# One stage for a whole gated recurrent mixer: norms, five projections, scan and output projection, batch by batch

## The chip, the core and the metric

The kernel runs on one core of a Trainium2 chip. TensorE (PE, with its weight loads PEld) multiplies matrices, VectorE (DVE), ScalarE (ACT) and GpSimd (POOL) work element by element, SyncE (SP) issues the transfers. Each engine runs its own instructions in order and waits on semaphores. The metric is the time of one execution on the device in microseconds.

## What is computed

The model has two layers of two mixers and a feed-forward part each, on x of 4 batches x 512 positions x 256 features. Every part is added to x after a layer norm. The change touches the second mixer of layer 2 alone:

```
xn = layernorm(x)                                   # the mixer's input, also its residual
y  = xn * rsqrt(mean(xn*xn) + 1e-5) * rms_w
f  = sigmoid(y @ Wf.T + bf)
z  = (y @ Wz.T) * sigmoid(y @ Wzg.T)
h_t = f_t * h_(t-1) + z_t                           # along the 512 positions, in bfloat16
gated = bfloat16(silu(y @ Wga.T) * (y @ Wgb.T)) * h
x  = x + gated @ Wout.T + bout + xn
```

## The kernel before

All activations stay in SBUF: X (rows: 128 positions x 16 tiles x 256 features, float32), XN (its norm) and XT (features on the partitions: 2 tiles x 2048 positions). A batch is 4 tiles of rows (TB), or 512 columns of XT. The kernel is a row of stages. Each `Stage` has its own buffers, semaphores and one block with a program for each engine; at its end the semaphores are cleared and all engines meet at a barrier, so nothing of a stage overlaps the next. Within an engine the order is the one written out by hand.

The mixer takes five stages (from the end of `hybrid_kernel`):

- `layer_norm` "ln7": VectorE takes statistics of a batch (L90, L93, L96), GpSimd the power -0.5 (L113), VectorE scales X into XN (L103), TensorE transposes it (L121) and ScalarE copies it into XT (L130). The mixer does not use this XT.
- `rms_scale`: VectorE squares XN (L1082), reduces all 16 tiles (L1084), GpSimd takes the power (L1077), VectorE scales XN into XR (L1089).
- `turn`: TensorE transposes XR (L397), ScalarE and VectorE copy the banks in turn (L406, L413).
- `recurrence`: SP loads the five weights, rms_w and the bias of f (L1117 to L1119). VectorE multiplies the transposed rows by rms_w (L1164). For each of eight units n (batch n // 2, half n % 2 of the 256 hidden features) TensorE makes five banks (f, z, z's gate, ga, gb), each of two float32 matmuls of 512 columns, which the trace shows as four records (L1138). ScalarE makes f and the two sigmoids (L1148, L1153); VectorE makes z (L1169), gg = ga * sigmoid(ga) (L1173) and gate (L1176). When all eight are done VectorE runs the eight scans (L1180) and products go (L1184), each copied to XT by ScalarE (L1156).
- `project_add` "r_out": SP loads the weight and the bias row (L428, L430). VectorE adds XN and then the bias to X (L448, L454), TensorE multiplies each tile of rows (L439), VectorE adds it (L459).

The helper class `Norm` is there already and used by another stage. Of it the change uses `statistics` and `scale`, which issue for one batch what L90 to L103 issue in `layer_norm`, with semaphores vare, rst and xn.

The experts' stage that follows (`moe2`) begins with a layer norm of X (lines L90 to L130 again).

Other lines named in the rows: L1734, L1782 are elementwise work of layer 2's first mixer, L2227 and L2263 too (L2227 a GpSimd product of two SBUF tiles, L2263 a VectorE product of two SBUF tiles), L814 the down projection of the shared expert.

Of the kernel before, what the change touches and what calls it, by code (L numbers as in the profile page):

```python
# [12 lines left out]
P = 128  # L13
# [1047 lines left out]

def rms_scale(nc, name, XN, XR, eps):

    with Stage(nc, name) as s:
        ms = s.sb("meansq", [P, NT])
        r = s.sb("r", [P, NT])
        mhalf = s.sb("mhalf", [P, NT])
        sq = s.sb("sq", [P, NT, DM])
        squared, msd, rd, out, half = (s.sem(n) for n in ("squared", "meansq", "r", "out", "half"))
        blk = s.block()  # L1070

        @blk.gpsimd
        def _(pool):
            nc.gpsimd.memset(mhalf[:, :], -0.5).then_inc(half, 1)
            pool.wait_ge(half, 1)
            pool.wait_ge(msd, 2)
            nc.gpsimd.tensor_tensor(r[:, :], ms[:, :], mhalf[:, :], ALU.pow).then_inc(rd, 1)  # L1077

        @blk.vector
        def _(dve):  # L1080
            for t in range(NT):
                nc.vector.tensor_tensor(sq[:, t, :], XN[:, t, :], XN[:, t, :], ALU.mult).then_inc(squared, 1)  # L1082
            dve.wait_ge(squared, NT)
            nc.vector.tensor_reduce(ms[:, :], sq[:, :, :], AX, ALU.add).then_inc(msd, 1)  # L1084
            dve.wait_ge(msd, 1)
            nc.vector.tensor_scalar(ms[:, :], ms[:, :], 1.0 / DM, eps, ALU.mult, ALU.add).then_inc(msd, 1)
            dve.wait_ge(rd, 1)
            for t in range(NT):
                nc.vector.tensor_scalar(XR[:, t, :], XN[:, t, :], r[:, t:t + 1], None, ALU.mult).then_inc(out, 1)  # L1089


def recurrence(nc, name, XRT, rms_w, w5, bf, GT):

# [4 lines left out]
    with Stage(nc, name) as s:  # L1098
        w = s.sb("w", [P, KT, 5 * DM])
        rw = s.sb("rms_w", [P, KT])  # L1100
        b_f = s.sb("bf", [P, 2])
        f = s.sb("f", [P, R, SEQ], BF16)
        z = s.sb("z", [P, R, SEQ], BF16)
        gate = s.sb("gate", [P, R, SEQ], BF16)
        h = s.sb("h", [P, R, SEQ], BF16)
        sig = s.sb("sig", [P, 2, 2, SEQ])
        gg = s.sb("gg", [P, 2, SEQ])
        go = s.sb("go", [P, R, SEQ], BF16)
        bank = [s.ps(f"bank{i}") for i in range(5)]
        ld, scaled, made, f_s, sig_s = (s.sem(n) for n in ("loaded", "scaled", "made", "f", "sig"))  # L1110
        zs, ggs, gs, steps, gos, outs = (s.sem(n) for n in ("z", "gg", "gate", "step", "go", "out"))
        blk = s.block()
        F_, Z, ZG, GA_, GB = range(5)

        @blk.sync
        def _(sp):
            sp.dma_start(w[:, :, :], tiles(w5)).then_inc(ld, 16)  # L1117
            sp.dma_start(rw[:, :], rms_w).then_inc(ld, 16)
            sp.dma_start(b_f[:, :], bf).then_inc(ld, 16)  # L1119
# [21 lines left out]

        @blk.scalar
        def _(act):
            act.wait_ge(ld, 48)
            for n in range(R):
# [8 lines left out]
            for n in range(R):  # L1154
                act.wait_ge(gos, n + 1)
                nc.scalar.copy(GT[:, n % 2, (n // 2) * SEQ:(n // 2 + 1) * SEQ], go[:, n, :]).then_inc(outs, 1)  # L1156

        @blk.vector
        def _(dve):
            dve.wait_ge(ld, 48)  # L1160
            for b in range(BATCH):
                for k in range(KT):
                    x = XRT[:, k, b * SEQ:(b + 1) * SEQ]
                    nc.vector.tensor_scalar(x, x, rw[:, k:k + 1], None, ALU.mult).then_inc(scaled, 1)  # L1164
            for n in range(R):
# [3 lines left out]
                nc.vector.tensor_tensor(z[:, n, :], bank[Z][:, :], sig[:, j, 0, :], ALU.mult).then_inc(zs, 1)  # L1169
                dve.wait_ge(sig_s, 2 * n + 2)  # L1170
                if n >= 2:
                    dve.wait_ge(gs, n - 1)
                nc.vector.tensor_tensor(gg[:, j, :], bank[GA_][:, :], sig[:, j, 1, :], ALU.mult).then_inc(ggs, 1)  # L1173
                dve.wait_ge(made, 5 * n + GB + 1)
                dve.wait_ge(ggs, n + 1)
                nc.vector.tensor_tensor(gate[:, n, :], gg[:, j, :], bank[GB][:, :], ALU.mult).then_inc(gs, 1)  # L1176
            for n in range(R):
                dve.wait_ge(f_s, n + 1)
                dve.wait_ge(zs, n + 1)
                nc.vector.tensor_tensor_scan(h[:, n, :], f[:, n, :], z[:, n, :], 0.0, ALU.mult, ALU.add  # L1180
                                             ).then_inc(steps, 1)
# [1323 lines left out]
```

## Time and profile before

| | |
|---|---|
| median of 3 runs | 4703.91 us (4699.47 to 4708.26) |
| the profiled execution | 4706.56 us, its span 4704.8 us |
| TensorE busy, share of the span | 4118.0 us, 88% |
| VectorE | 2696.7 us, 57% |
| ScalarE | 2268.6 us, 48% |
| GpSimd | 630.6 us, 13% |
| mean granted clock of TensorE | 0.919 of full speed |

Times in the trace are microseconds from the start of the span. A float32 matmul shows as two records, each with a weight load. "x20" behind a row means that 20 instructions in a row are merged, and what stands in square brackets is the idle time before it and what ended it. A record's length includes its way through the engine, so that the next of the same kind can start earlier: what a row of them costs is the distance of their starts.

### The profile page before, as it was taken

The numbers are of one execution on the slowest core, as the hardware profiler recorded it, in microseconds if no ns is written. First come the engines' busy times: TensorE is split into PE (matmuls) and PEld (weight loads), VectorE is DVE, ScalarE is ACT, GpSimd is POOL, SyncE is SP. The second block draws the span as 40 slices with busy tenths as digits, with TensorE's granted clock in tenths as the row PEclk, the third lists the DMA queues.
The fourth block names the chain that finished last, engine by engine and source line by source line (L and its number), as shares of the span: only waits on it lengthen the run. The fifth ranks groups of instructions, "written<-read, shape, count | busy, mean of one in ns | idle before, by whom it ended". The sixth has DMA issues, their size and how long they took to land. (4 is left out here: it accounts for less than half of the span.)

```text
span 4704.8 us, 79644 instructions
## 1 busy us (share of the span) xinstructions
PE 4118.0 (88%) x27938; PEld 2752.2 (58%) x27938; DVE 2696.7 (57%) x7063; ACT 2268.6 (48%) x6183; POOL 630.6 (13%) x557
## 2 busy tenths in 40 slices
PE   5988988888797799959999999999999999977667
PEld 3555545555555566646666666666766666644344
DVE  3663357777623788856666665566556666423342
ACT  1551146666411566635556555656565565522111
POOL 0000010000000344421111111111111111111011
PEclk8788989889897899979999999999999999979879
DMA  2000100000000655553222332333233232121012
GB/s 70 1 1 24 51 1 2 2 2 2 4 27 5 206 200 205 213 134 84 79 70 74 84 84 71 81 84 83 70 84 84 66 80 79 37 92 57 11 34 76
DMA packets 402161, 318.92 MB, mean 68 GB/s; under 512 B 289200, under 2 KB 339056, under 8 KB 399728
## 3 DMA queue, kind: packets, MB, share of 16 engines
q1 hardware_dynamic: 398704, 305.53, 22.6%
q0 software_dynamic: 3072, 8.39, 0.6%
q8 instruction: 225, 3.69, 0.3%
q14 instruction: 160, 1.31, 0.1%
HBM read 195.94 MB, written 117.88 MB: 67 GB/s over the span
## 5 line engine op out<-in xcount | busy, mean ns | idle before, releaser
L2153 ACT ACTIVATE d_heads_VP<-d_heads_chain,d_GALL 128x128 f32<-128x128 f32 x512 | 187.9, 367 | 665.1 <-PE d_heads_chain L2055 663.5
L2299 DVE SCALAR_TENSOR_TENSOR d_heads_S<-d_heads_S,d_GALL,d_heads_chain 128x128 f32<-128x128 f32 x768 | 232.4, 344 | 436.0 <-PE d_heads_chain L2060 435.9
L599 ACT ACTIVATE b_heads_PR<-b_heads_sc,b_heads_NM 128x384 f32<-128x384 f32 (+3 forms) x512 | 273.0, 535 | 203.4 <-DVE b_heads_NM L667 203.4
L1763 DVE SCALAR_TENSOR_TENSOR d_front_CY<-d_front_proj,d_CW,d_front_CY 128x511 f32<-128x511 f32 (+2 forms) x384 | 274.1, 745 | 72.6 <-ACT d_front_CY L1681 68.0
L1969 PE MATMUL d_heads_value<-all_XT,d_heads_WVZ 128*128 128x512 f32 x512 | 271.1, 612 | 27.9 <-DMA d_heads_WVZ<-w_d_qkvz 27.9
L2232 POOL TENSOR_TENSOR d_heads_RM<-d_heads_MS,d_heads_mhalf 128x4 f32<-128x4 f32 x128 | 130.4, 1019 | 1199.9 <-DVE d_heads_MS L2312 1199.9
L2277 DVE SCALAR_TENSOR_TENSOR d_heads_CY<-d_heads_value,d_CW,d_heads_CY 128x511 f32<-128x511 f32 (+2 forms) x384 | 284.6, 741 | 1.8
L1990 PE MATMUL d_heads_value<-d_heads_WVZ,all_XT 128*128 128x256 f32 x1024 | 273.6, 390 | 12.0 <-DVE d_heads_CY L2277 12.0
L2087 PE MATMUL d_heads_projected<-d_heads_WO,d_heads_OT 128*128 128x256 f32 x1024 | 277.0, 394 | 0.7 <-ACT d_heads_OT L2172 0.7
L2060 PE MATMUL d_heads_chain<-d_heads_VP,d_heads_KD 64*128 64x128 f32 x1792 | 220.4, 322 | 54.2 <-ACT d_heads_VP L2153 54.1
L2291 DVE SCALAR_TENSOR_TENSOR d_heads_UU<-d_heads_chain,d_GALL,d_heads_VB 128x128 f32<-128x128 f32 x448 | 156.5, 349 | 192.9 <-PE d_heads_chain L2042 192.9
L547 PEld LDWEIGHTS b_heads_tp<-all_ident,b_heads_PR 128*128 128x128 f32 x1280 | 158.0, 156 | 170.7 <-ACT b_heads_PR L599 129.1
L2042 PE MATMUL d_heads_chain<-d_heads_S,d_heads_KQ 128*64 128x128 f32 x1792 | 249.3, 302 | 8.5 <-DVE d_heads_S L2299 2.4
L547 PE MATMUL b_heads_tp<-all_ident,b_heads_PR 128*128 128x128 f32 x1280 | 223.6, 311 | 37.2 <-DVE b_heads_PT L679 24.3
L1639 PE MATMUL d_front_proj<-all_XT,d_front_WKQ 128*128 128x512 f32 x512 | 242.4, 618 | 15.3 <-DMA d_front_WKQ<-w_d_qkvz 15.3
L2065 PE MATMUL d_heads_output<-d_heads_VP,d_heads_ITB 128*128 128x128 f32 x1024 | 244.4, 321 | 0.0
L538 PE MATMUL b_heads_sc<-b_QKT,b_heads_QM 32*128 32x128 f32 (+3 forms) x1024 | 229.3, 527 | 17.0 <-DVE b_heads_QM L635 8.9
L2060 PEld LDWEIGHTS d_heads_chain<-d_heads_VP,d_heads_KD 64*128 64x128 f32 x1792 | 134.8, 184 | 176.9 <-ACT d_heads_VP L2153 163.7
L2227 POOL TENSOR_TENSOR d_heads_QS<-d_heads_KQ,d_heads_GE 128x512 f32<-128x512 f32 x128 | 162.9, 1274 | 517.2 <-PE d_heads_output L2065 510.8
L2045 PE MATMUL d_heads_output<-d_heads_S,d_heads_QS 128*64 128x128 f32 x1792 | 226.8, 282 | 0.0
L2263 DVE TENSOR_TENSOR d_heads_TMP<-d_heads_INV 128x30 f32<-128x30 f32 (+14 forms) x480 | 209.5, 437 | 28.5 <-DMA d_heads_INV<-d_l 25.1
L2042 PEld LDWEIGHTS d_heads_chain<-d_heads_S,d_heads_KQ 128*64 128x64 f32 x1792 | 126.7, 136 | 158.5 <-DVE d_heads_S L2299 56.2
(323 smaller groups left out, 8932.3 us busy)
## 6 DMA issues: line engine op xcount, KB each, us to landing
d_kq<-d_front_KQ SPq DMA_DIRECT2D x64, 768.0 KB, 4.3
d_heads_KQ<-d_kq SPq DMA_DIRECT2D x64, 768.0 KB, 4.9
d_heads_GE<-d_gerows SPq DMA_DIRECT2D x128, 256.0 KB, 5.3
d_front_GR<-d_grows SPq DMA_DIRECT2D x32, 512.0 KB, 6.4
d_it<-d_front_LI SPq DMA_DIRECT2D x64, 256.0 KB, 2.1
d_l<-d_front_LI SPq DMA_DIRECT2D x64, 256.0 KB, 4.0
d_heads_ITB<-d_it SPq DMA_DIRECT2D x128, 128.0 KB, 2.8
d_heads_INV<-d_l SPq DMA_DIRECT2D x256, 32.0 KB
```

The source lines that it names most:

```text
L547: mm = nc.tensor.transpose(TP[j][:, k * P:(k + 1) * P], PR[p % 3][j][:, k * P:(k + 1) * P], C.ident[:, :])
L599: nc.scalar.activation(PR[p % 3][j][:, 0:width(p)], SC[p % 2][j][:, 0:width(p)], ACT.Exp, bias=NM[:, u % 2, t, slot:slot + 1], scale=-1.0 ...
L1639: mm = nc.tensor.matmul(FB[2 * (i % 2) + c][:, :], WKQ[:, k, g, col:col + HD], XT[:, k, b * SEQ:(b + 1) * SEQ], start=(k == 0), stop=(k == ...
L1763: stt(y, FB[2 * (i % 2) + c][:, 0:SEQ - j], CW[:, n, 3 - j:4 - j], y, ALU.mult, ALU.add).then_inc(convstep if j < 3 else convs, 1)
L1969: mm = nc.tensor.matmul(BV[h][:, :], w[:, k, h * HD:(h + 1) * HD], XT[:, k, b * SEQ:(b + 1) * SEQ], start=(k == 0), stop=(k == KT - 1))
L1990: mm = nc.tensor.matmul(BV[t // 2][:, (t % 2) * DM:(t % 2 + 1) * DM], XT[:, k, b * SEQ + t * P:b * SEQ + (t + 1) * P], w[:, k, 2 * HD:4 * HD],
L2042: mm = nc.tensor.matmul(R[0][hrows(h), 0:HD], kq[:, c, 0, :], S[:, h, :], start=True, stop=True)
L2060: mm = nc.tensor.matmul(R[h][:, HD:2 * HD], KD[i % 2][hrows(h), c, :], VP[c % 2][hrows(h), :], start=True, stop=True)
L2065: mm = nc.tensor.matmul(inter, ITB[i % 2][:, c, :], VP[c % 2][:, :], start=(c == 0), stop=True, skip_group_check=True)
L2087: mm = nc.tensor.matmul(BO[:, t * DM:(t + 1) * DM], OT[:, h, t * P:(t + 1) * P], WO[g % 2][:, h, :], start=(h == 0), stop=(h == 1))
L2277: stt(y, BV[h][:, 0:SEQ - j], CW[:, 2 * HK + 2 * g + h, 3 - j:4 - j], y, ALU.mult, ALU.add).then_inc(convstep if j < 3 else convs, 1)
L2299: stt(S[:, h, :], S[:, h, :], gate(i, GEL0 + h, c), R[h][:, HD:2 * HD], ALU.mult, ALU.add).then_inc(su, 1)
```

## The change

`gated_scan` replaces the five stages. All of it is one stage with one block, and its order goes by batches. Both norms are made of the statistics of X: with variance v and r = 1/sqrt(v + 1e-5) the mean square of the normed row is v * r * r, so the second factor is (v r r + 1e-5)^-0.5, and XR = (X - mean) * (r * factor) comes straight from X. XN is still made, for the residual. rms_w is ScalarE's scale in the copy of the transposed rows. The two adds of the residual and the bias go to GpSimd, one batch behind the norms. The scan of a unit stands in VectorE's order between its gg and its gate; the output projection of a batch stands behind the projections of the next one, two tiles of rows in a bank of PSUM, added with one instruction. TensorE has one bank for each of the five projections as before, two for the transposes and one for the output.

Lines that are only "..." stand for what is left out, the bodies of the two removed functions above all (they are in the kernel before).

```diff
     return M
-def rms_scale(nc, name, XN, XR, eps):
...
+def gated_scan(nc, name, X, XN, GT, W, C):
+    R = 2 * BATCH
     with Stage(nc, name) as s:
...
+        w, wo = s.sb("w", [P, KT, 5 * DM]), s.sb("w_out", [P, KT, DM])
+        rw, b_f, b_o = s.sb("rms_w", [P, KT]), s.sb("bf", [P, 2]), s.sb("bias", [P, DM])
+        XR, XRT = s.sb("rows", [P, NT, DM]), s.sb("rows_turned", [P, KT, NT * P])
+        SQ, RR, RS = (s.sb(n, [P, NT]) for n in ("meansq", "root", "factor"))
+        f, z, gate, h, go = (s.sb(n, [P, R, SEQ], BF16) for n in ("f", "z", "gate", "h", "go"))
+        sig, gg = s.sb("sig", [P, 2, 2, SEQ]), s.sb("gg", [P, 2, SEQ])
+        xp = [s.ps(f"xp{i}") for i in range(2)]
+        bank = [s.ps(f"bank{i}") for i in range(5)]
+        ob = s.ps("out_bank")
+        N = Norm(nc, s, X, XN, None, C, xp)
+        (wl, bl, ol, tiny, sqd, rrd, rsd, xr, turned, copied, made, f_s, sig_s, zs, ggs, gs, steps, gos, outs, op, added, biased,
+         res) = (s.sem(n) for n in (
+             "weights_loaded", "bias_loaded", "out_loaded", "tiny", "meansq", "root", "factor", "rows", "turned", "copied", "made",
+             "f", "sig", "z", "gg", "gate", "scanned", "gated", "go_copied", "out_made", "added", "biased", "residual"))
         blk = s.block()
+        F_, Z, ZG, GA_, GB = range(5)
+        out_bank = lambda u: xp[0] if u == 2 * BATCH - 1 else ob
+        @blk.sync
+        def _(sp):
+            sp.dma_start(w[:, :, :], tiles(W["r_w5"])).then_inc(wl, 16)
+            sp.dma_start(rw[:, :], W["rms_w"]).then_inc(bl, 16)
+            sp.dma_start(b_f[:, :], W["Wf_b"]).then_inc(bl, 16)
+            sp.dma_start(b_o[:, :], W["r_out_bias"].broadcast_to([P, DM])).then_inc(ol, 16)
+            sp.dma_start(wo[:, :, :], tiles(W["r_out"])).then_inc(ol, 16)
         @blk.gpsimd
         def _(pool):
...
-def recurrence(nc, name, XRT, rms_w, w5, bf, GT):
...
+            nc.gpsimd.memset(N.mhalf[:, :], -0.5).then_inc(N.half, 1)
+            pool.wait_ge(N.half, 1)
+            def residual(b):
+                own = slice(b * TB, (b + 1) * TB)
+                pool.wait_ge(N.xn, TB * (b + 1))
+                pool.wait_ge(xr, TB * (b + 1))
+                pool.wait_ge(ol, 32)
+                nc.gpsimd.tensor_tensor(XN[:, own, :], XN[:, own, :], b_o[:, :].unsqueeze(1).broadcast_to([P, TB, DM]), ALU.add
+                                        ).then_inc(biased, 1)
+                pool.wait_ge(biased, b + 1)
+                nc.gpsimd.tensor_tensor(X[:, own, :], X[:, own, :], XN[:, own, :], ALU.add).then_inc(res, 1)
+            for b in range(BATCH):
+                own = slice(b * TB, (b + 1) * TB)
+                pool.wait_ge(N.vare, b + 1)
+                nc.gpsimd.tensor_tensor(N.rstd[:, own], N.var[:, own], N.mhalf[:, own], ALU.pow).then_inc(N.rst, 1)
+                pool.wait_ge(sqd, b + 1)
+                nc.gpsimd.tensor_tensor(RR[:, own], SQ[:, own], N.mhalf[:, own], ALU.pow).then_inc(rrd, 1)
+                if b >= 1:
+                    residual(b - 1)
+            residual(BATCH - 1)
         @blk.tensor
         def _(pe):
...
-            for n in range(R):
...
+            def turn_rows(b):
+                pe.wait_ge(xr, TB * (b + 1))
+                for k in range(KT):
+                    if b > 0:
+                        pe.wait_ge(copied, 2 * (b - 1) + k + 1)
+                    for t in range(TB):
+                        mm = nc.tensor.transpose(xp[k][:, t * P:(t + 1) * P], XR[:, TB * b + t, k * P:(k + 1) * P],
+                                                 C.ident[:, :])
+                    mm.then_inc(turned, 1)
+            def project_five(n):
+                b, j = divmod(n, 2)
+                pe.wait_ge(copied, 2 * (b + 1))
                 for q in range(5):
                     if n > 0:
                         if q == F_:
                             pe.wait_ge(f_s, n)
-                        elif q in (Z, ZG):
+                        elif q == Z:
                             pe.wait_ge(zs, n)
+                        elif q == ZG:
+                            pe.wait_ge(sig_s, 2 * n - 1)
                         elif q == GA_:
                             pe.wait_ge(ggs, n)
                         else:
@@ -1139,10 +1147,42 @@
                                               XRT[:, k, b * SEQ:(b + 1) * SEQ], start=(k == 0), stop=(k == KT - 1))
                     mm.then_inc(made, 1)
+            def project_out(u):
+                pe.wait_ge(outs, 2 * (u // 2 + 1))
+                pe.wait_ge(ol, 32)
+                if u == 2 * BATCH - 1:
+                    pe.wait_ge(copied, 2 * BATCH)
+                else:
+                    pe.wait_ge(added, u)
+                for i in range(2):
+                    t = 2 * u + i
+                    for k in range(KT):
+                        mm = nc.tensor.matmul(out_bank(u)[:, i * DM:(i + 1) * DM], GT[:, k, t * P:(t + 1) * P], wo[:, k, :],
+                                              start=(k == 0), stop=(k == KT - 1))
+                mm.then_inc(op, 1)
+            turn_rows(0)
+            pe.wait_ge(wl, 16)
+            for b in range(BATCH):
+                project_five(2 * b)
+                if b + 1 < BATCH:
+                    turn_rows(b + 1)
+                if b >= 1:
+                    project_out(2 * b - 2)
+                project_five(2 * b + 1)
+                if b >= 1:
+                    project_out(2 * b - 1)
+            project_out(2 * BATCH - 2)
+            project_out(2 * BATCH - 1)
         @blk.scalar
         def _(act):
...
-            for n in range(R):
+            def copy_rows(b):
+                for k in range(KT):
+                    act.wait_ge(turned, 2 * b + k + 1)
+                    nc.scalar.activation(XRT[:, k, b * SEQ:(b + 1) * SEQ], xp[k][:, :], ACT.Copy, scale=rw[:, k:k + 1]
+                                         ).then_inc(copied, 1)
+            def gates(n):
                 j = n % 2
                 act.wait_ge(made, 5 * n + F_ + 1)
                 nc.scalar.activation(f[:, n, :], bank[F_][:, :], ACT.Sigmoid, bias=b_f[:, j:j + 1]).then_inc(f_s, 1)
@@ -1151,37 +1191,78 @@
                     if n >= 2:
                         act.wait_ge(zs if i == 0 else ggs, n - 1)
                     nc.scalar.activation(sig[:, j, i, :], bank[q][:, :], ACT.Sigmoid).then_inc(sig_s, 1)
-            for n in range(R):
+            def copy_gated(n):
                 act.wait_ge(gos, n + 1)
                 nc.scalar.copy(GT[:, n % 2, (n // 2) * SEQ:(n // 2 + 1) * SEQ], go[:, n, :]).then_inc(outs, 1)
+            act.wait_ge(bl, 32)
+            copy_rows(0)
+            for b in range(BATCH):
+                gates(2 * b)
+                if b + 1 < BATCH:
+                    copy_rows(b + 1)
+                if b >= 1:
+                    copy_gated(2 * b - 1)
+                gates(2 * b + 1)
+                copy_gated(2 * b)
+            copy_gated(R - 1)
         @blk.vector
         def _(dve):
...
-            for n in range(R):
+            def norm(b):
+                own = slice(b * TB, (b + 1) * TB)
+                N.statistics(dve, b)
+                dve.wait_ge(N.rst, b + 1)
+                nc.vector.tensor_tensor(SQ[:, own], N.rstd[:, own], N.rstd[:, own], ALU.mult).then_inc(tiny, 1)
+                dve.wait_ge(tiny, 2 * b + 1)
+                nc.vector.tensor_tensor(SQ[:, own], SQ[:, own], N.mv[:, own, 1], ALU.mult).then_inc(tiny, 1)
+                dve.wait_ge(tiny, 2 * b + 2)
+                nc.vector.tensor_scalar_add(SQ[:, own], SQ[:, own], 1e-5).then_inc(sqd, 1)
+                N.scale(dve, b)
+                dve.wait_ge(rrd, b + 1)
+                nc.vector.tensor_tensor(RS[:, own], RR[:, own], N.rstd[:, own], ALU.mult).then_inc(rsd, 1)
+                dve.wait_ge(rsd, b + 1)
+                for t in range(b * TB, (b + 1) * TB):
+                    nc.vector.tensor_scalar(XR[:, t, :], X[:, t, :], N.mv[:, t, 0:1], RS[:, t:t + 1], ALU.subtract, ALU.mult
+                                            ).then_inc(xr, 1)
+            def gates(n):
                 j = n % 2
                 dve.wait_ge(made, 5 * n + Z + 1)
                 dve.wait_ge(sig_s, 2 * n + 1)
                 nc.vector.tensor_tensor(z[:, n, :], bank[Z][:, :], sig[:, j, 0, :], ALU.mult).then_inc(zs, 1)
+                dve.wait_ge(made, 5 * n + GA_ + 1)
                 dve.wait_ge(sig_s, 2 * n + 2)
                 if n >= 2:
                     dve.wait_ge(gs, n - 1)
                 nc.vector.tensor_tensor(gg[:, j, :], bank[GA_][:, :], sig[:, j, 1, :], ALU.mult).then_inc(ggs, 1)
+                dve.wait_ge(f_s, n + 1)
+                dve.wait_ge(zs, n + 1)
+                nc.vector.tensor_tensor_scan(h[:, n, :], f[:, n, :], z[:, n, :], 0.0, ALU.mult, ALU.add).then_inc(steps, 1)
                 dve.wait_ge(made, 5 * n + GB + 1)
                 dve.wait_ge(ggs, n + 1)
                 nc.vector.tensor_tensor(gate[:, n, :], gg[:, j, :], bank[GB][:, :], ALU.mult).then_inc(gs, 1)
-            for n in range(R):
...
                 dve.wait_ge(gs, n + 1)
                 dve.wait_ge(steps, n + 1)
                 nc.vector.tensor_tensor(go[:, n, :], gate[:, n, :], h[:, n, :], ALU.mult).then_inc(gos, 1)
+            def add(u):
+                dve.wait_ge(res, u // 2 + 1)
+                dve.wait_ge(op, u + 1)
+                x = X[:, 2 * u:2 * u + 2, :].rearrange("p t n -> p (t n)")
+                nc.vector.tensor_tensor(x, x, out_bank(u)[:, :], ALU.add).then_inc(added, 1)
+            norm(0)
+            for b in range(BATCH):
+                if b + 1 < BATCH:
+                    norm(b + 1)
+                gates(2 * b)
+                if b >= 1:
+                    add(2 * b - 2)
+                gates(2 * b + 1)
+                if b >= 1:
+                    add(2 * b - 1)
+            add(2 * BATCH - 2)
+            add(2 * BATCH - 1)
@@ -2417,14 +2498,7 @@
             M.load = None
-            layer_norm(nc, "ln7", X, XN, XT, C)
-            with Stage(nc, "r") as a:
-                XR = a.sb("XR", [P, NT, DM])
-                rms_scale(nc, "r_rms", XN, XR, 1e-5)
-                XRT = a.sb("XRT", [P, KT, NT * P])
-                turn(nc, "r_turn", XR, XRT, C)
-                recurrence(nc, "r_scan", XRT, W["rms_w"], W["r_w5"], W["Wf_b"], XT)
-            project_add(nc, "r_out", X, XT, W["r_out"], bias_row=W["r_out_bias"], residual=XN)
+            gated_scan(nc, "r", X, XN, XT, W, C)
             experts(nc, "moe2", X, XN, XT, W, M, C)
         store_x(nc, X, out)
```

## Rows read from the trace of the kernel before

**Rows 1.** the page's head

```profile
span 4704.8 us, 79644 instructions
```

**Rows 2.** the table by stretches (us, busy time (x instructions) of each engine, clock, DMA)

```profile
4337.50:4389.10 51.60, 13.86 (x65) 12.49 (x65) 32.74 (x98) 7.04 (x12) 7.89 (x7) 0.53 0.07 26
4389.10:4460.60 71.50, 71.46 (x160) 31.19 (x160) 15.87 (x24) 16.33 (x25) 0.00 (x0) 0.96 0.00 0
4460.60:4496.10 35.50, 15.50 (x64) 13.11 (x64) 28.75 (x41) 4.94 (x8) 0.00 (x0) 0.76 0.05 12
```

**Rows 3.** timeline from 4337 us (start, length, engine, line, operation)

```profile
4337.52 1.41 DVE L90 BATCH_NORM_STATS2 ln_stats<-all_X 128x6 f32<-128x256 f32 x4 [0.95 <-PEq L40]
...
4339.57 1.05 POOL L113 TENSOR_TENSOR ln_rstd<-ln_var,ln_mhalf 128x4 f32<-128x4 f32 x1 [1.97 <-DVE ln_var L96]
...
4341.11 1.38 DVE L103 TENSOR_SCALAR all_XN<-all_X,ln_meanvar,ln_rstd 128x256 f32<-128x256 f32 x4
...
4344.54 0.59 ACT L130 COPY all_XT<-ln_xp 128x512 f32<-128x512 f32 x1 [0.27 <-PE ln_xp L121]
```

**Rows 4.** DMA issues from 4337 to 4497 us (KB, us to landing)

```profile
r_scan_w<-w_r_w SPq DMA_DIRECT2D x1, 1280.0 KB, 5.5
```

**Rows 5.** groups of instructions from 4337 to 4497 us (busy us, mean ns)

```profile
L1138 PE MATMUL r_scan_bank<-r_XRT,r_scan_w 128*128 128x512 f32 x160 | 71.5, 610 | 10.8 <-DVE r_XRT L1164 10.8
...
L439 PE MATMUL r_out_bank<-r_out_w,all_XT 128*128 128x256 f32 x64 | 15.5, 407 | 19.6 <-DMA r_out_bias<-w_r_out_bias 19.6
...
L1156 ACT CAST all_XT<-r_scan_go 128x512 f32<-128x512 bf16 x8 | 4.9, 618 | 10.8 <-DVE r_scan_go L1184 10.8
```

**Rows 6.** timeline of TensorE's weight loads from 4389 us

```profile
4392.61 0.34 PEld L1138 LDWEIGHTS r_scan_bank<-r_XRT,r_scan_w 128*128 128x128 f32 x1 [0.52 <-issue]
4393.47 0.34 PEld L1138 LDWEIGHTS r_scan_bank<-r_XRT,r_scan_w 128*128 128x128 f32 x1 [0.52 <-issue]
4394.31 0.19 PEld L1138 LDWEIGHTS r_scan_bank<-r_XRT,r_scan_w 128*128 128x128 f32 x1 [0.50 <-issue]
```

**Rows 7.** timeline of the old turn's bank copies from 4374.5 us

```profile
4376.54 0.59 ACT L406 COPY r_XRT<-r_turn_bank 128x512 f32<-128x512 f32 x1 [1.12 <-PE r_turn_bank L397]
4377.39 0.69 DVE L413 COPY r_XRT<-r_turn_bank 128x512 f32<-128x512 f32 x1 [1.01 <-PE r_turn_bank L397]
4377.82 0.59 ACT L406 COPY r_XRT<-r_turn_bank 128x512 f32<-128x512 f32 x1 [0.70 <-PE r_turn_bank L397]
```

**Rows 8.** timeline of VectorE from 4459 us

```profile
4459.51 0.69 DVE L1173 TENSOR_TENSOR r_scan_gg<-r_scan_bank,r_scan_sig 128x512 f32<-128x512 f32 x1 [0.95 <-ACT r_scan_sig L1153]
4460.60 0.69 DVE L1176 TENSOR_TENSOR r_scan_gate<-r_scan_gg,r_scan_bank 128x512 bf16<-128x512 f32 x1 [0.40 <-PE r_scan_bank L1138]
4461.20 1.22 DVE L1180 TENSOR_TENSOR_SCAN r_scan_h<-r_scan_f,r_scan_z 128x512 bf16<-128x512 bf16 x1
4462.53 0.43 DVE L1184 TENSOR_TENSOR r_scan_go<-r_scan_gate,r_scan_h 128x512 bf16<-128x512 bf16 x1
```

**Rows 9.** timeline of GpSimd and VectorE from 3005 us

```profile
3005.74 1.27 POOL L2227 TENSOR_TENSOR d_heads_QS<-d_heads_KQ,d_heads_GE 128x512 f32<-128x512 f32 x1
3006.04 1.01 DVE L2263 TENSOR_TENSOR d_heads_TMP<-d_heads_INV 128x30 f32<-128x30 f32 x1
...
3009.25 0.21 DVE L2263 TENSOR_TENSOR d_heads_TMP<-d_heads_INV 128x58 f32<-128x58 f32 x1
```

**Rows 10.** timeline from 1752 us, and line L113 by min/median/max ns

```profile
1752.10 4.05 POOL L1734 TENSOR_TENSOR d_front_LI<-d_front_LI,d_front_NB 128x512 f32<-128x512 f32 x4
...
1753.66 1.28 DVE L1782 TENSOR_TENSOR d_front_LI<-d_front_kk,d_front_D 128x512 f32<-128x512 f32 x2
...
L113 POOL TENSOR_TENSOR ln_rstd<-ln_var,ln_mhalf x4: 1047/1244/1247, 4339.6 to 4347.4; 128x4 f32<-128x4 f32 x4
```

**Rows 11.** timeline of TensorE from 4325 us

```profile
4325.27 1.13 PE L814 MATMUL moe_bank<-moe_shared_down,moe_hid 128*128 128x256 f32 x4 [0.54 <-DVE all_X L999]
4329.50 2.07 PE L814 MATMUL moe_bank<-moe_shared_down,moe_hid 128*128 128x256 f32 x4 [3.10 <-issue]
```

More of the change, by code:

```diff
@@ L1059, in expert_weights @@
     return M
-def rms_scale(nc, name, XN, XR, eps):
+def gated_scan(nc, name, X, XN, GT, W, C):
+    R = 2 * BATCH
     with Stage(nc, name) as s:
[L1065 to L1069, printed above, removed]
-        blk = s.block()
+        w, wo = s.sb("w", [P, KT, 5 * DM]), s.sb("w_out", [P, KT, DM])
[12 more added lines that the diff above has]
+             "f", "sig", "z", "gg", "gate", "scanned", "gated", "go_copied", "out_made", "added", "biased", "residual"))
+        blk = s.block()
+        F_, Z, ZG, GA_, GB = range(5)
[7 more added lines that the diff above has]
+            sp.dma_start(wo[:, :, :], tiles(W["r_out"])).then_inc(ol, 16)
@@ L1072, in _ @@
         @blk.gpsimd
         def _(pool):
[L1074 to L1089, printed above, removed]
@@ L1092, in recurrence @@
-def recurrence(nc, name, XRT, rms_w, w5, bf, GT):
-    R = 2 * BATCH
[L1098 to L1119, printed above, removed]
+            nc.gpsimd.memset(N.mhalf[:, :], -0.5).then_inc(N.half, 1)
@@ L1122, in _ @@
         def _(pe):
-            pe.wait_ge(ld, 48)
-            pe.wait_ge(scaled, R)
-            for n in range(R):
-                b, j = n // 2, n % 2
+            def turn_rows(b):
[7 more added lines that the diff above has]
+                    mm.then_inc(turned, 1)
@@ L1140, in _ @@
                     mm.then_inc(made, 1)
+            def project_out(u):
[24 more added lines that the diff above has]
+            project_out(2 * BATCH - 1)
         @blk.scalar
         def _(act):
-            act.wait_ge(ld, 48)
-            for n in range(R):
+            def copy_rows(b):
[4 more added lines that the diff above has]
+            def gates(n):
                 j = n % 2
@@ L1153, in _ @@
                     nc.scalar.activation(sig[:, j, i, :], bank[q][:, :], ACT.Sigmoid).then_inc(sig_s, 1)
-            for n in range(R):
+            def copy_gated(n):
                 act.wait_ge(gos, n + 1)
                 nc.scalar.copy(GT[:, n % 2, (n // 2) * SEQ:(n // 2 + 1) * SEQ], go[:, n, :]).then_inc(outs, 1)
+            act.wait_ge(bl, 32)
[9 more added lines that the diff above has]
+            copy_gated(R - 1)
         @blk.vector
         def _(dve):
[L1160 to L1164, printed above, removed]
-            for n in range(R):
+            def norm(b):
[15 more added lines that the diff above has]
+            def gates(n):
                 j = n % 2
@@ L1176, in _ @@
                 nc.vector.tensor_tensor(gate[:, n, :], gg[:, j, :], bank[GB][:, :], ALU.mult).then_inc(gs, 1)
-            for n in range(R):
[L1178 to L1181, printed above, removed]
                 dve.wait_ge(gs, n + 1)
```

## The prediction

> **What bounds the kernel now.** I read the page's head first: the profiled execution spans 4704.8 us [rows 1]. Then the table by stretches. The changed mixer is three stretches of 158.6 us in all [rows 2]: 51.6 us from the first statistics of its layer norm to the first projection matmul, 71.5 us of projections, 35.5 us from the last projection to the last add. In the first TensorE is busy 13.9 us and VectorE 32.7, in the third TensorE is busy 15.5 and VectorE 28.7: no engine is full there, the stages stand one behind the other. In the middle TensorE is busy 71.46 of 71.50 us: that is a floor. The other 4546 us of the kernel aren't touched. So the question is how much of 51.6 + 35.5 = 87.1 us goes beside the 71.5 us, and what TensorE work comes into its path in return.
>
> **The front.** I take the timeline of the old norm as the pattern [rows 3]. Statistics of a batch and their pow on GpSimd: 4337.52 to 4340.62, so 3.1 us. New behind it: three chained tiny VectorE instructions; the small ones in this trace cost 0.17 to 0.21 us, I take 0.2 each, 0.6. Then the second pow, 1.24 us, beside which the four XN scalings run (1.38 us for four [rows 3]); RS, another 0.2; the four scalings into XR, 1.4, as they have the form of the XN ones; all with hops 3.6. That puts XR of batch 0 at 6.7 us. From the last XN to the second ScalarE copy the old timeline takes 4342.49 to 4345.13, 2.65 us [rows 3], eight transposes among it; the copy now carries rms_w as its scale, which takes the eight multiplies (L1164) away. First projection matmul at 9.4 us instead of 51.55: 42.1 us saved. The four stage boundaries that go are within these stretches. Cover: the weights (1280 KB, 5.5 us to landing [rows 4]) are issued at the stage's start and needed at 9.4; if they came after that, every us would show. SP issues the same five transfers, all at the start; nothing else is queued on SP behind them in this stage, and the output weights are needed only some 40 us in. The 16 adds of X and XN, and of the bias (L448, L454), move to GpSimd.
>
> **The middle.** All 160 projection records stay: 71.5 us [rows 5]. They start at the low clock now, with weight loads of 0.34 us and 0.86 us from one to the next up to 4393.47, then 0.19 us and 0.43 [rows 6]: six records at 1.2 instead of 2.4 GHz, 2.6 us. I leave that in. A group of ten matmuls (20 records) then takes 20 x 0.429 = 8.6 us. New in TensorE's order before the last projection: 24 transposes and the output projections of units 0 to 4. The old turn's late banks come 0.43 us apart (4377.39 to 4377.82 [rows 7]) for four transposes each, so 0.107 each, 2.6 us for 24. The output projection issued 64 records in 15.1 us, 13.8 us at the full clock (0.216 each) and 1.3 for its slow start [rows 5]; a unit is 8 records, 1.72 us, five are 8.6. Price: 11.2 us. On this path the ScalarE work is two copies and one gated copy between the last transpose of a batch and the output unit behind it, 0.6 us each with overlaps and hops, 1.4 us of TensorE waiting, in batches 1 and 2 (in batch 3 there are no rows to copy and the gated copy is early): 2.8 us.
>
> **The tail.** M is when the last bank is made. The last gg begins at M - 1.09, the scan (1.22 us) now runs before the gate, ending at M + 0.75; gate and go as in the rows (0.69 with the next starting 0.6 later, 0.43) end at M + 1.85 [rows 8]; the gated copy, 0.62 [rows 5], at M + 2.5; units 6 and 7, 1.72 each, to M + 6.2; the last add, a 512-column one at 0.69, at M + 6.9. Seven further scans, go's, copies and adds, which the old tail ran here, lie beside TensorE. 35.5 - 6.9 = 28.6 us saved.
>
> **Where VectorE stands in the way.** Its order is norm(b+1) before gates(2b). Behind norm(b+1) wait its own gates, and TensorE's turn_rows(b+1), which comes after the five projections of unit 2b. A norm is 6.7 us (above). In loop 1 it starts when gates(1) is done, M1 + 1.85, ends at M1 + 8.6, and TensorE arrives at M1 + 8.4: 0.2 us. In loop 2 it starts behind add(1), 0.9 us after TensorE began unit 4, and ends at 7.6 of 8.6 us: hidden by 1 us. Norm(1) is hidden too: TensorE's first unit, 11.2 us long with its slow start, ends at 20.6 and the rows are there at 13.4. So far 42.1 + 28.6 - 11.2 - 2.8 - 0.2 = 56.5 us.
>
> **GpSimd against VectorE.** Right after the second pow of norm(b+1) GpSimd runs residual(b): two 128x1024 instructions, both reading SBUF, at the very time when RS and XR are due. The trace shows what that does [rows 9]: a VectorE product of 30 columns with two SBUF inputs begins 0.3 us after a GpSimd 128x512 one and takes 1.01 us, to 3007.05, when GpSimd has just ended (3007.01); 58 columns with GpSimd idle take 0.21. Instructions with one input in PSUM aren't held: L1782 runs at 0.64 us apiece beside GpSimd's [rows 10]. And the small pow takes 1.05 us beside statistics but 1.24 beside the XN scalings [rows 10], so the tensor_scalar form is in it as well. The Trainium skill, SBUF — State Buffer, Who interferes with whom, says that the pair of ports is locked for a whole instruction by whichever of GpSimd and a 2-port or two-SBUF-input VectorE instruction is first. By that rule, the trace agrees for the two-input form (1.01 against 0.2 us). Price: 512 columns on GpSimd take 1.01 us in place [rows 10] to 1.27 with two full inputs [rows 9], so the bias add is 2.0 and the X add 2.5: RS waits for the first, XR for the second, the norm grows by 4.4 us. Bounds: 0 (GpSimd starts later or doesn't hold it) and 5.1 (both 2.5). TensorE then waits 4.6 us before turn_rows(2) and 3.4 before turn_rows(3); norm(1) ends at 17.8, still hidden by 2.8. Taken: 8.0 - 0.2 = 7.8 us. And a wait of that length costs the clock: after 0.54 us idle four L814 records take 1.13 us, after 3.10 us idle 2.07 [rows 11]. A slow start costs 1.3 (output projection) to 2.6 us (projections): I take 1.3 twice, as transposes begin it. 2.6 us; the ends are 0 and 5.2. Residual(3) meets gates(4) and holds scan and go by 2 us, which nobody needs for 7 us: nothing.
>
> The Trainium skill, TensorE: Matmul & The Clock Gate, Part 4: PE-mode transpose, holds that transposes don't lift the clock. The old turn speaks against it: only transposes had run, and its late banks come at 0.43 us instead of 0.85 (4376.54 to 4377.39) [rows 7]. By the rule the first projections start as slow as now (what the sum has); by the row up to 0.9 us less.
>
> **Sum.** 56.5 - 7.8 - 2.6 = 46.1 us. The execution shown took 4706.6 us around its span of 4704.8 and lies 2.7 above the median of the runs, 4703.9. So 4660.5 by its own time, and 4658 beside the median.
>
> **The rivals.**
> - The ports hold less than I count: only RS is held (2.0 us a norm), not XR, or GpSimd comes later. TensorE waits 2 and 1 us, the clock stays up: 52 to 56 us, 4648 to 4652. For it: the two-scalar form's 0.345 us a piece is as slow as a two-input one (1.38 for four), so it may be no 2-port instruction; against it: the pow at 1.24 us. 0.34.
> - The norms aren't hidden: each of batches 1 to 3 costs TensorE its whole 6.7 + 4.4 = 11.1 us instead of 8.0 in all, 33.3 - 8 = 25 us more: 4683. VectorE has 6.7 + 4.4 + 2 x 3.7 + 1.3 = 19.8 us of work in a batch of 21.5 for TensorE, so one more hold of 2 us would fill it. 0.06.
> - Slower than before: TensorE's clock. The place is the wait before turn_rows(2); if the records behind it stay at 1.2 GHz, as they do now through the first six, each of 120 projection records costs 0.43 us more, 51 us, and outputs and transposes 16: 4658 + 67 = 4725. It decides from 108 slow projection records on. For it: what an idle stretch did to L814 [rows 11]; against it: six records sufficed [rows 6], and 8.6 us without a gap lie between the waits. 0.03.
> - It doesn't do what it says: the rows of the stages that follow or the code's own loading take back all of it. Nothing in the trace points there. 0.01.
>
> **How the numbers follow.** My case 0.56 (4653 to 4668: GpSimd at 2 or 2.5, slow starts 0 to 5.2), the first rival 0.34, the second 0.06, the others 0.04. The range has to hold the first two and part of the third: from 4640 (56.5 us, a first start at full clock, and the 4.4 us by which the runs differ) to 4674. 0.2%, about what a measurement of this kernel can tell from no change, is 9.4 us: faster 0.95, same 0.02, slower 0.03.
>
> **What would show it.** First projection 9.4 us after the first statistics; the last add 6.9 us after the last bank; the stage about 112 us instead of 158.6; bias and X adds on GpSimd at 2.0 and 2.5 us with RS and XR longer beside them; TensorE idle some 4.6 and 3.4 us before turn_rows(2) and (3), with 0.34 us weight loads or transposes 0.21 apart behind. Waits under 1 us there make my port step wrong; a stage over 125 us makes the overlap wrong.

## The result and the profile after

The kernel takes 4655.35 us (median of four runs, 4645.13 to 4662.02) against 4701.69 of before beside it: ratio 0.9899, 95% interval 0.9876 to 0.9922. That is 46 us less. The forecast was 4658 us, its range 4640 to 4674.

The profiled execution has a span of 4660.2 us where [rows 1] had 4704.8, 44.6 us less. The mixer itself went from 158.6 us [rows 2] to 114.9. The 0.9 us between the two are the sum of larger differences in stages that nobody touched: the mixer starts 3.1 us later than before (4340.63 against 4337.52), the experts' stage behind it is 4.3 us shorter (203.7 against 208.0), and so is the one ahead of the mixer (194.2 against 198.5), which the change can't reach. Single executions differ by that much, so the experiments below are read by the mixer's own length, from the start of its first statistics to the end of its last add. Where an experiment says "the stage", that is meant.

The page's head and the table by stretches, cut at the same three events as [rows 2] (first projection, last bank made, last add):

```profile
span 4660.2 us, 79489 instructions
...
PE 4116.7 (88%) x27906; PEld 2752.5 (59%) x27906; DVE 2687.4 (58%) x7033; ACT 2263.5 (49%) x6179; POOL 650.4 (14%) x567
...
4340.60:4350.10 9.50, 1.97 (x8) 1.57 (x8) 6.95 (x30) 1.45 (x3) 3.36 (x4) 0.50 0.54 180
4350.10:4448.40 98.30, 89.00 (x225) 45.60 (x226) 57.71 (x97) 23.82 (x38) 24.86 (x14) 0.89 0.00 0
4448.40:4455.60 7.20, 5.42 (x25) 4.14 (x23) 3.87 (x6) 0.62 (x1) 0.00 (x0) 1.00 0.00 0
```

Front and tail shrank from 51.6 and 35.5 us to 9.5 and 7.2; the middle grew from 71.5 to 98.3 us, and TensorE is busy in only 89.0 of them. What stands in the 98.3 is in TensorE's timeline (start, length, line, operation; in brackets the idle time before and what ended it):

```profile
4347.31 1.97 PE L1126 MATMUL r_xp<-all_ident,r_rows 128*128 128x128 f32 x8 [15.11 <-DVE r_rows L1226]
4350.15 10.71 PE L1146 MATMUL r_bank<-r_rows_turned,r_w 128*128 128x512 f32 x20 [0.87 <-ACT r_rows_turned L1182]
4360.70 1.04 PE L1126 MATMUL r_xp<-all_ident,r_rows 128*128 128x128 f32 x8
4361.57 17.33 PE L1146 MATMUL r_bank<-r_rows_turned,r_w 128*128 128x512 f32 x40
4382.78 1.97 PE L1126 MATMUL r_xp<-all_ident,r_rows 128*128 128x128 f32 x8 [3.88 <-DVE r_rows L1226]
4386.04 3.78 PE L1160 MATMUL r_out_bank<-r_w_out,all_XT 128*128 128x256 f32 x8 [1.28 <-ACT all_XT L1197]
4389.61 9.69 PE L1146 MATMUL r_bank<-r_rows_turned,r_w 128*128 128x512 f32 x20
...
4412.41 1.97 PE L1126 MATMUL r_xp<-all_ident,r_rows 128*128 128x128 f32 x8 [2.80 <-DVE r_rows L1226]
4415.67 3.54 PE L1160 MATMUL r_out_bank<-r_w_out,all_XT 128*128 128x256 f32 x8 [1.28 <-ACT all_XT L1197]
...
4448.24 1.89 PE L1160 MATMUL r_out_bank<-r_w_out,all_XT 128*128 128x256 f32 x8
```

The two long waits are those before turn_rows(2), 3.88 us, and turn_rows(3), 2.80 us, both for XR. Behind each the eight transposes take 1.97 us instead of 1.04, and the output unit of eight records 3.78 and 3.54 us instead of 1.89. The table by stretches shows the clock behind it: 0.50 of full speed, the lower of its two levels, from 4381.3 to 4391.5 and from 4412.0 to 4418.8 us, and 1.00 between the two. Why XR is late stands in VectorE's and GpSimd's rows of the same norm:

```profile
4345.68 0.16 DVE L1223 TENSOR_TENSOR r_factor<-r_root,r_ln_rstd 128x4 f32<-128x4 f32 x1
4345.88 1.38 DVE L1226 TENSOR_SCALAR r_rows<-all_X,r_ln_meanvar,r_factor 128x256 f32<-128x256 f32 x4
...
4375.60 1.38 DVE L160 TENSOR_SCALAR all_XN<-all_X,r_ln_meanvar,r_ln_rstd 128x256 f32<-128x256 f32 x4
4377.05 2.17 DVE L1223 TENSOR_TENSOR r_factor<-r_root,r_ln_rstd 128x4 f32<-128x4 f32 x1
4379.25 3.48 DVE L1226 TENSOR_SCALAR r_rows<-all_X,r_ln_meanvar,r_factor 128x256 f32<-128x256 f32 x4
...
4375.77 1.25 POOL L1113 TENSOR_TENSOR r_root<-r_meansq,r_ln_mhalf 128x4 f32<-128x4 f32 x1 [0.68 <-DVE r_meansq L1220]
4376.84 2.35 POOL L1104 TENSOR_TENSOR all_XN<-all_XN,r_bias 128x1024 f32<-128x1024 f32 x1
4379.27 2.34 POOL L1107 TENSOR_TENSOR all_X<-all_X,all_XN 128x1024 f32<-128x1024 f32 x1
```

In batch 0, where GpSimd has nothing to add, RS takes 0.16 us and the four XR instructions 1.38. In batch 2 RS begins 0.2 us behind the bias add and ends 4379.22, as that does (4379.19); XR's first begins with the X add (4379.25 and 4379.27) and the four take 3.48 us, of which the longest alone takes 2.52 us where 0.40 is usual. The XN scalings just ahead take 1.38 us, beside the pow.

### The profile page after: what moved, and what is told of

It reads as the page before. It is cut to its first block and busy times, and to the rows that moved or that the text cites. A ratio compares the mean times of both kernels' runs of the same rounds, so it can differ in the third digit from the quotient of the medians.

```text
span 4660.2 us, 79489 instructions
## 1 busy us (share of the span) xinstructions
PE 4116.7 (88%) x27906; PEld 2752.5 (59%) x27906; DVE 2687.4 (58%) x7033; ACT 2263.5 (49%) x6179; POOL 650.4 (14%) x567
```

## The experiments

All of them start from the changed kernel. Run e8 was timed four times; of the others the stage's length in one profiled execution is read. The first unit, which e1 to e7 leave as it is, took 10.22 to 10.86 us in these executions and that of the changed kernel, so that some tenths of a microsecond say nothing.

### e1: the adds behind XR

```diff
                 if b >= 1:
+                    pool.wait_ge(xr, TB * (b + 1))
                     residual(b - 1)
```

> GpSimd's two adds of residual(b-1) wait for the four XR instructions of batch b; nothing else differs. Theory (the ports): RS falls from 2.17 to about 0.17 us, the four XR from 3.48 to 1.38 us, TensorE waits under 0.3 us before turn_rows(2) and turn_rows(3) instead of 3.88 and 2.80, so the clock stays up and the 3.5 + 2.5 us of slow records behind the waits go too: the stage is 114.9 - 6.5 - 6.0 = 102.5 us, from the first statistics to the last add. Rival (the norm is late by itself, through VectorE's order, and GpSimd doesn't hold it): RS, XR, both waits and 114.9 us stay within 1 us.

The stage took 102.26 us. VectorE, GpSimd and TensorE in the norm of batch 2 and behind it:

```profile
4367.23 0.17 DVE L1224 TENSOR_TENSOR r_factor<-r_root,r_ln_rstd 128x4 f32<-128x4 f32 x1
4367.43 1.38 DVE L1227 TENSOR_SCALAR r_rows<-all_X,r_ln_meanvar,r_factor 128x256 f32<-128x256 f32 x4
...
4369.92 2.40 DVE L1242 TENSOR_TENSOR_SCAN r_h<-r_f,r_z 128x512 bf16<-128x512 bf16 x1
...
4368.88 2.36 POOL L1104 TENSOR_TENSOR all_XN<-all_XN,r_bias 128x1024 f32<-128x1024 f32 x1 [1.69 <-DVE r_rows L1227]
4371.32 3.15 POOL L1107 TENSOR_TENSOR all_X<-all_X,all_XN 128x1024 f32<-128x1024 f32 x1
...
4368.91 1.04 PE L1127 MATMUL r_xp<-all_ident,r_rows 128*128 128x128 f32 x8
4371.38 1.99 PE L1161 MATMUL r_out_bank<-r_w_out,all_XT 128*128 128x256 f32 x8 [1.43 <-ACT all_XT L1198]
```

RS 0.17, XR 1.38, no wait before the transposes, and these and the unit at the full clock: the granted clock is 1.00 from 4354.5 us to the end of the stage. The hold by GpSimd's adds is the cause of both waits. It has moved on to the scan, 2.40 us instead of 1.22, where nobody waits for it. GpSimd's X add, which meets the scan, is lengthened too, 3.15 instead of 2.34 us. The rival, a norm that is late by itself, is out.

### e2: the gated copy first

```diff
-                if b + 1 < BATCH:
-                    copy_rows(b + 1)
                 if b >= 1:
                     copy_gated(2 * b - 1)
+                if b + 1 < BATCH:
+                    copy_rows(b + 1)
```

> On ScalarE the gated copy of unit 2b-1 goes ahead of the two copies of the turned rows; nothing else differs. Theory: the 1.28 us that TensorE waits between a batch's transposes and the output unit behind them (twice) are these three ScalarE instructions in a row; both waits fall under 0.2 us and the stage goes from 114.9 to about 112.4 us, the waits of 3.9 and 2.8 us before turn_rows and the slow records stay. Rival: the output unit waits for something else (VectorE's add of the unit before), and 114.9 us stay.

The stage took 108.41 us, 6.5 less and not 2.5. TensorE:

```profile
4378.89 1.97 PE L1126 MATMUL r_xp<-all_ident,r_rows 128*128 128x128 f32 x8 [3.88 <-DVE r_rows L1226]
4380.65 3.62 PE L1160 MATMUL r_out_bank<-r_w_out,all_XT 128*128 128x256 f32 x8
...
4405.98 1.09 PE L1126 MATMUL r_xp<-all_ident,r_rows 128*128 128x128 f32 x8 [2.79 <-DVE r_rows L1226]
4406.91 1.89 PE L1160 MATMUL r_out_bank<-r_w_out,all_XT 128*128 128x256 f32 x8
```

Both 1.28 us waits are gone, as expected: the units follow the transposes at once. Most of the other 3.9 us is clock. In batch 2 it fell during the wait as before and was back after 6.8 us instead of 10.2, which gives 1.0 us. In batch 3, behind a wait of 2.79 us and as long as before, transposes and unit run fast (1.09 and 1.89 us) and the granted clock stays at 1.00, which gives 2.5 us.

The edit doesn't explain the second part. In the changed kernel the clock fell 2.4 us into that wait, before the transposes ran; the 1.28 us behind them, which this edit takes away, came later. e6 below has two more waits of this length (2.72 and 2.73 us) with transposes at 1.09 us behind. Each kernel was profiled once, so what the edit itself is worth lies between the 2.6 us of its waits and the 6.5 us measured.

### e3 and e4: the waits filled

```diff
             def turn_rows(b):
+                if b >= 2:
+                    pe.wait_ge(copied, 2 * b)
+                for i in range({2: 34, 3: 24}.get(b, 0)):
+                    nc.tensor.transpose(xp[0][:, (i % TB) * P:(i % TB + 1) * P], C.ident[:, :], C.ident[:, :])
                 pe.wait_ge(xr, TB * (b + 1))
```

> TensorE issues 34 transposes of the identity into a free bank before it waits for the rows of batch 2 and 24 before those of batch 3 (3.6 and 2.6 us of work at 0.107 us each, inside the waits of 3.88 and 2.80 us); the rows come no earlier. It separates the wait from the clock. Theory (the slow records behind the waits are the price of an idle TensorE, and transposes count as work): turn_rows at 0.107 us a transpose, output units at 1.72 us, the stage 114.9 - 6.0 = 109 us. Rival (a page's rule that transposes don't keep the clock up): the records behind stay slow, 3.5 and 2.5 us of extra time, 115 us. If the clock cost me nothing here: 115 us too, but with fast records.

In e4 the loop runs 4 and 3 times over one matmul, `nc.tensor.matmul(xp[0][:, :], C.ident[:, :], XRT[:, 0, 0:SEQ], start=True, stop=True)`.

> As the run before, but with four and three real matmuls of 512 columns (3.4 and 2.6 us) in place of the transposes. Theory: the clock stays at 2.4 GHz through both waits, the records behind are fast, the stage is 109 us; both theories on transposes agree here, so this gives the clock's price by itself. Against it: if the records behind are slow for another reason than the idle time, 115 us.

The stage took 110.92 us with the transposes and 110.91 with the matmuls. TensorE of e3 in both batches, then batch 3 of e4:

```profile
4369.38 3.88 PE L1124 MATMUL r_xp<-all_ident 128*128 128x128 f32 x34
4373.44 1.09 PE L1130 MATMUL r_xp<-all_ident,r_rows 128*128 128x128 f32 x8 [0.19 <-DVE r_rows L1230]
4375.96 1.99 PE L1164 MATMUL r_out_bank<-r_w_out,all_XT 128*128 128x256 f32 x8 [1.42 <-ACT all_XT L1201]
...
4396.69 2.78 PE L1124 MATMUL r_xp<-all_ident 128*128 128x128 f32 x24
4399.67 1.09 PE L1130 MATMUL r_xp<-all_ident,r_rows 128*128 128x128 f32 x8 [0.20 <-DVE r_rows L1230]
4402.19 3.43 PE L1164 MATMUL r_out_bank<-r_w_out,all_XT 128*128 128x256 f32 x8 [1.43 <-ACT all_XT L1201]
```

```profile
4390.82 1.10 PE L1130 MATMUL r_xp<-all_ident,r_rows 128*128 128x128 f32 x8 [0.23 <-DVE r_rows L1230]
4393.34 3.40 PE L1164 MATMUL r_out_bank<-r_w_out,all_XT 128*128 128x256 f32 x8 [1.43 <-ACT all_XT L1201]
```

The rows come no earlier (the filler of e3 ends 0.19 and 0.20 us ahead of them), so the 4.0 us gained are clock alone. In batch 2 all of it came back: transposes 1.09, unit 1.99 us. In batch 3 the transposes are fast and the unit behind its wait of 1.4 us is slow again, in both runs alike: 2 us short of the 6 that I expected. Transposes did as well as matmuls in every place. In e3 the granted clock is 1.00 through both rows of them and falls at 4402.5, when the unit has already begun.

The rule of the Trainium skill that I set against the old turn (TensorE: Matmul & The Clock Gate, Part 4: PE-mode transpose) does not hold here. The plainest case is e8: TensorE did nothing but float32 transposes from 4337.70 on, and its granted clock rose from 0.50 to 1.00 at 4340.7. In the kernel before it rose at 4377.3, when only the old turn's transposes had run since 4372.00.

### e5: each norm one batch ahead

```diff
             norm(0)
+            norm(1)
             for b in range(BATCH):
-                if b + 1 < BATCH:
-                    norm(b + 1)
                 gates(2 * b)
+                if b + 2 < BATCH:
+                    norm(b + 2)
```

> VectorE runs norm(0) and norm(1) first and then norm(b+2) behind gates(2b), so each norm is a batch early; GpSimd's adds stay where they hold RS and XR. Theory (the holds cost only because norm(b+1) is due at once): RS 2.2 and XR 3.5 us stay, the waits before turn_rows vanish and the clock stays up, but gates(1) comes late behind norm(2): TensorE waits some 2 us for z of unit 1, and 0.5 us for an add in batch 1: the stage is 105 us, near the 102.3 of the run with the adds moved. Rival (what counts is the hold itself): no better than 112.

The stage took 106.48 us. No wait before the transposes; the one place where TensorE waits long is the expected one:

```profile
4366.27 8.83 PE L1146 MATMUL r_bank<-r_rows_turned,r_w 128*128 128x512 f32 x16 [1.91 <-DVE r_z L1233]
4374.94 1.04 PE L1126 MATMUL r_xp<-all_ident,r_rows 128*128 128x128 f32 x8
```

1.91 us for z of unit 1, and the 16 records behind it take until 4374.94, 8.7 us where 16 x 0.43 = 6.9 are due. The granted clock fell at 4366.8, half a microsecond after the work had begun again, and was back at 4370.1. That slow start accounts for the 1.5 us by which I was under. So a held norm no longer delays its own rows when they aren't due at once. It isn't free: z of unit 1 stands behind norm(2) in VectorE's order, and the 4.1 us for which GpSimd holds that norm are more than the 1.91 us that TensorE waits for z.

### e6: the tail undone

The scans, `go`, gated copies and output units stand behind the last projection on their engines (VectorE: two scans of a batch, then the adds of the batch before); the rest is as changed. TensorE's part of the edit:

```diff
-                if b >= 1:
-                    project_out(2 * b - 2)
                 project_five(2 * b + 1)
-                if b >= 1:
-                    project_out(2 * b - 1)
-            project_out(2 * BATCH - 2)
-            project_out(2 * BATCH - 1)
+            for u in range(2 * BATCH):
+                project_out(u)
```

> One part undone: scans, products, gated copies and output units all stand behind the last projection, as they did before; norms, turns and projections stay batch by batch. Theory: the projections end some 12 us sooner (no five output units of 1.72 us, no two waits of 1.28, part of the slow records moved), at about 95 us, and behind them each output unit with its add is a chain of 2.7 us, eight of them behind the first two scans: about 27 us, so 122 us instead of 114.9. By my sum's tail term read alone (28.6 us saved less 8.6 of units put into the middle) it would be 135.

The stage took 120.47 us, 5.5 more than in the changed kernel. TensorE's first two units behind the projections, and the last but one:

```profile
4421.23 3.78 PE L1160 MATMUL r_out_bank<-r_w_out,all_XT 128*128 128x256 f32 x8 [4.75 <-ACT all_XT L1193]
4425.95 3.58 PE L1160 MATMUL r_out_bank<-r_w_out,all_XT 128*128 128x256 f32 x8 [0.94 <-DVE all_X L1249]
...
4444.13 1.97 PE L1160 MATMUL r_out_bank<-r_w_out,all_XT 128*128 128x256 f32 x8 [0.94 <-DVE all_X L1249]
```

Projections end 88.3 us into the stage, and 32 us of scans, copies and units follow. The units wait 0.94 us for the add of the one before or, where a new batch begins, 1.96 us for its gated copy. Most of what the tail's overlap gives is paid back in the middle. The 5.5 us are a net figure with the waits as they fell in these two executions: in e6 the waits before turn_rows(2) and (3) were 2.72 and 2.73 us with no fall of the clock, and the first two units ran slowly behind the wait of 4.75 us. What this overlap is worth without GpSimd's holds wasn't run.

### e7: all norms first

```diff
-            norm(0)
             for b in range(BATCH):
-                if b + 1 < BATCH:
-                    norm(b + 1)
+                norm(b)
+            for b in range(BATCH):
                 gates(2 * b)
```

> The other part undone in VectorE's order: all four norms before the first gates. Theory: norm(3) ends at 6.6 + 3 x 10.5 = 38 us, z of unit 0 at 38.8 instead of 18.2, TensorE waits 16 us in its second unit and starts slow behind it (2 us), the waits of 3.9 and 2.8 us before turn_rows and the slow records behind them vanish: 114.9 + 16 + 2 - 6.7 - 6 = 120 us. Rival (the chain of projections alone sets the end, whatever VectorE does first): 103 to 108 us.

```profile
4371.58 18.34 PE L1146 MATMUL r_bank<-r_rows_turned,r_w 128*128 128x512 f32 x36 [15.95 <-DVE r_z L1233]
```

The stage took 120.98 us; TensorE waits 15.95 us for the first z, and its next records start slowly. Both long waits before the transposes are gone. That VectorE makes its norms beside the projections is thus worth 6 us as the kernel stands. RS and XR are held in this run too, so it doesn't say what the order is worth without the holds.

### e8: what the runs add up to

e1 and e2 together, and TensorE is kept at work while it waits for the first rows:

```diff
+            for i in range(36):
+                nc.tensor.transpose(xp[0][:, (i % TB) * P:(i % TB + 1) * P], C.ident[:, :], C.ident[:, :])
             turn_rows(0)
```

> GpSimd's adds behind XR (as in e1), the gated copy first (as in e2), and 36 transposes of the identity on TensorE at the stage's start, while it waits for the first rows. Theory: 102.3 - 2 x 1.4 - 1.9 (first unit fast) - 0.9 (first transposes fast) = 96.7 us for the stage, 18 us less than the change as made: the kernel near 4637 us against 4702 before, ratio 0.986. If transposes don't count as work: 99.5 us, first unit 10.7 us as before.

```profile
4337.70 5.61 PE L1165 MATMUL r_xp<-all_ident 128*128 128x128 f32 x36 [8.43 <-PEq L40]
4344.38 1.09 PE L1127 MATMUL r_xp<-all_ident,r_rows 128*128 128x128 f32 x8 [1.07 <-DVE r_rows L1229]
4346.55 8.82 PE L1147 MATMUL r_bank<-r_rows_turned,r_w 128*128 128x512 f32 x20 [1.08 <-ACT r_rows_turned L1185]
...
4373.25 1.04 PE L1127 MATMUL r_xp<-all_ident,r_rows 128*128 128x128 f32 x8
4374.12 1.89 PE L1161 MATMUL r_out_bank<-r_w_out,all_XT 128*128 128x256 f32 x8
```

The stage took 96.17 us. The first unit takes 8.82 us instead of 10.71, with nothing but transposes ahead of it. The kernel takes 4637.33 us (median of four runs) against 4700.15: ratio 0.9862, 95% interval 0.9844 to 0.9880. The intervals of this and of the change as made just overlap in their comparisons with before; by the profiled stages the difference is 18.8 us, by the medians 18.0.

## Why the prediction was right

The time was right, and so was the sign of each term. That the two medians differ by 46.3 us where 46.1 were forecast is luck: the mixer itself gave 43.7 us, the four runs of the changed kernel spread over 17 us, and stages that nobody touched differ by 4 us between two executions. Inside the mixer, too, terms that came out too high and one that came out too low partly cancel. By the prediction's steps:

- **The front.** First projection at 9.4 us; it came at 9.52. XR of batch 0 was ready at 6.6 against 6.7. The pattern of the old norm's timeline carried over instruction by instruction.
- **The middle's price.** Transposes at 0.107 us and units at 1.72 are what the fast ones take. The first unit lost 2.0 us to its slow start instead of 2.6. The wait for three ScalarE instructions, forecast at 1.4 us twice, was 1.28 twice; in e2, where the gated copy goes first, it is gone.
- **The tail.** Forecast 6.9 us behind the last bank, measured 7.15.
- **GpSimd against VectorE.** The waits were to be 4.6 and 3.4 us and were 3.88 and 2.80: GpSimd's two adds took 2.34 us each (2.0 and 2.5 in the sum), and the hold came to 4.1 us a norm, not 4.4. e1 shows that nothing else makes them. The rival in which only RS is held is out by XR's 3.48 against 1.38 us. The rule of the Trainium skill (SBUF — State Buffer, Who interferes with whom) agrees with both, the two-input form (RS ends 0.03 us after the bias add) and the tensor_scalar, which that page counts among the forms that can take both ports (XR's first, 2.52 us). That instruction and the X add begin within 0.02 us of each other, so the rows don't show which was issued first. Residual(3) held scan and go by 1.2 and 1.4 us (2 forecast), and no one waited for it.
- **The clock: the term that was mis-sized.** "I take 1.3 twice": 2.6 us. Measured against e1, where the same records are fast: transposes +0.9, unit +1.7, projections behind it +0.95 in batch 2 (3.6 us), +0.9 and +1.5 in batch 3 (2.5 us), together 6.1 us. It lay beyond the upper end that I gave, 5.2. The mis-sized step was to take the slow start of a stream of output records, 1.3 us, as the price of each wait. In its place the clock fell to 0.50 while TensorE was still waiting and stayed there for 10.2 and 6.8 us: through the transposes, the 1.28 us of waiting behind them and the unit, and in batch 2 into the projections.
- **Where the errors went.** Ports 1.3 us less than the sum had, ScalarE's wait 0.2 and the first slow start 0.6 less, the clock 3.5 more: 1.4 of the 2.4 us by which the stage (114.9) exceeds the forecast (112.5). Front and tail are 0.4 more, and 0.6 is left in small gaps.
- **Slower by the clock.** The full clock was back 8.7 and 6.4 us after the two waits ended, and nothing near 108 projection records stayed slow. **Norms not hidden** was forced in e7: 120.98 us.

What stays open is which idle stretches cost the clock. The granted clock of each run, read in steps of 0.1 us (full speed before and after):

| run and place | TensorE's wait | clock falls to 0.50 | clock back |
|---|---|---|---|
| changed kernel, batch 2 | 3.88 us, to 4382.78 | 4381.3 | 4391.5 |
| changed kernel, batch 3 | 2.80 us, to 4412.41 | 4412.0 | 4418.8 |
| e2, batch 2 | 3.88 us, to 4378.89 | 4377.4 | 4384.2 |
| e2, batch 3 | 2.79 us, to 4405.98 | stays at 1.00 | |
| e6, batches 2 and 3 | 2.72 and 2.73 us | stays at 1.00 | |
| e5, unit 1 | 1.91 us, to 4366.27 | 4366.8 | 4370.1 |
| e3, unit of batch 3 | 0.20 us, eight transposes, 1.43 us, to 4402.19 | 4402.5 | 4406.0 |
| e3, unit of batch 2 | 0.19 us, eight transposes, 1.42 us | stays at 1.00 | |

e4 goes as e3, and e1 keeps the full clock through two waits of 1.43 us. So the length of a wait doesn't decide it alone: 1.9 us cost the clock once, and 2.7 to 2.8 us did not in three cases of four. The runs don't show what does.

## What to carry to other kernels

When stages are merged so that one engine's work hides another's, list for each moved instruction who runs beside it in SBUF: two GpSimd adds moved off VectorE's list held just the VectorE instructions that TensorE waited for, and one wait instruction that moved them a little later was worth 12.7 us in the stage, against 43.7 for the whole merge. A wait of TensorE costs its length and can cost its clock; for the upper end of a range price the records behind it at the low clock for as long as it lasted here, 6.4 and 8.7 us past the wait. Overlap has to be counted net: taking the tail's scans and output units into the middle was worth 5.5 us as the kernel stands, not the 28.6 that my sum has for the shorter tail.

## What I had not expected

- An output unit at the low clock behind only 0.2 and 1.4 us of idleness (3.4 instead of 1.99 us, e3 and e4), where the same pattern a batch earlier stayed fast.
- GpSimd's X add grows from 2.34 to 3.15 us when it meets VectorE's scan (e1 and batch 3 of the changed kernel): GpSimd is held as well.
- Putting one ScalarE copy ahead of two others, for 2.6 us of waiting, went with 6.5 us less in the one execution profiled; 2.5 us of them are a fall of the clock that did not come, for no reason that the rows show.
- 36 transposes of the identity, 5.6 us of work in an otherwise idle stretch, took 1.9 us off the first unit: in this kernel, filling TensorE's idle time ahead of a stream paid.
